# Moving 64 value matmuls of the cross attention from the last layer's network stage into the recurrence of the first layer

## The reference

```python
x = _layernorm(x + _L0_attn_ref(x, ...))        # selective state-space recurrence
x = _layernorm(x + _L0_xattn_ref(x, ctx, ctx))  # autocorrelation
x = _layernorm(x + _L0_ffn_ref(x, ...))         # quantized weights and LoRA
x = _layernorm(x + _L1_attn_ref(x, ...))        # 4-layer network with a scan
x = _layernorm(x + _L1_xattn_ref(x, ctx, ...))  # grouped-query cross attention
x = _layernorm(x + _L1_ffn_ref(x, ...))         # routed low-rank experts
```

```python
k_, v_ = jnp.split(kv @ Wkv + bkv, 2, axis=-1)   # kv = ctx; 8 heads of 128 each
```

## Time and profile before

| | us |
|---|---|
| time, median of 3 runs (1371.46 to 1374.9) | 1371.84 |
| span of the profiled execution | 1371.0 |
| PE busy | 1271.2 |
| DVE busy | 920.7 |
| ACT busy | 731.0 |
| POOL busy | 646.6 |
| recurrence: first scan starts, last scan ends | 136.7, 488.0 |
| network: first L801, last L835 starts | 673.0, 809.5 |
| first scores of the attention (L931) | 846.7 |

### The profile page before, as it was taken

One profiled execution on the slowest core, in us unless ns is written; L12 is line 12 of the kernel. 1 busy time (PEld: TensorE's weight loads), 2 busy tenths in 40 slices (PEclk: granted clock), 3 DMA queues, 4 the chain that ended last, 5 costly groups with the idle time before them and its releaser, 6 DMA issues.

```text
span 1371.0 us, 18309 instructions
## 1 busy us (share of the span) xinstructions
PE 1271.2 (93%) x6432; PEld 923.8 (67%) x6432; DVE 920.7 (67%) x1690; ACT 731.0 (53%) x1407; POOL 646.6 (47%) x471
## 2 busy tenths in 40 slices
PE   6996888888889989999999999999998999999996
PEld 5875766666677754444655556778787888888774
DVE  4774999999999877886644544544444464555566
ACT  5479999999998831112222234544444435444441
POOL 4128999999989702216511123533332543333221
PEclk9998899999999999999999999999999999999998
DMA  5002200040000060002110002212121222221110
GB/s 180 9 25 93 93 1 1 32 153 2 1 1 0 1 187 16 8 9 92 70 31 8 15 24 70 93 62 77 63 77 46 70 77 72 69 68 63 39 54 31
DMA packets 29641, 71.45 MB, mean 52 GB/s; under 512 B 3408, under 2 KB 3664, under 8 KB 27632
## 3 DMA queue, kind: packets, MB, share of 16 engines
q1 hardware_dynamic: 29552, 70.30, 15.6%
HBM read 68.12 MB, written 2.16 MB: 51 GB/s over the span
## 4 chain that ended last, share of the span: by engine, by line
PE 69%; DVE 10%; POOL 9%; issue 6%; ACT 4%; DMA 1%; DVEq 0%; SPq 0%; POOLq 0%; ACTq 0%
PE psum L502 10%; PE psum L504 9%; PE psum L503 9%; POOL arena L1420 8%; PE psum L931 4%; PE psum L791 4%; PE psum L958 4%; DVE arena L1696 4%; PE psum L785 3%; PE psum L602 3%; PE psum L577 3%; ACT arena L983 3%; PE psum L591 2%; PE psum L688 2%; PE psum L672 2%
## 5 line engine op out<-in xcount | busy, mean ns | idle before, releaser
L1356 POOL TENSOR_TENSOR w_split<-arena,w_split 128x512 fp32r<-128x512 f32 x128 | 168.0, 1331 | 315.1 <-ACT w_split L983 315.1
L1420 POOL TENSOR_TENSOR arena<-arena 128x1024 f32<-128x1024 f32 x128 | 300.4, 2373 | 28.3 <-DVE arena L1696 28.1
L1696 DVE TENSOR_TENSOR_SCAN arena<-psum,arena 128x512 f32<-128x512 f32 x256 | 290.6, 1200 | 15.7 <-ACT psum L983 15.5
L577 PE MATMUL psum<-prm,arena 128*128 128x128 f32 x1024 | 159.0, 284 | 59.1 <-DVE arena L1696 31.1
L577 PEld LDWEIGHTS psum<-prm,arena 128*128 128x128 f32 x1024 | 114.5, 143 | 121.1 <-issue 53.7
L983 ACT ACTIVATE arena<-psum,ssmC 128x256 f32<-128x256 f32 x448 | 179.9, 497 | 16.7 <-PE psum L577 16.6
L983 ACT ACTIVATE arena<-arena 128x512 f32<-128x512 f32 (+2 forms) x86 | 64.1, 749 | 224.9 <-DVE arena L1979 224.0
L983 ACT ACTIVATE psum<-arena,amat 128x508 f32<-128x508 f32 x256 | 172.3, 727 | 10.0 <-DVE arena L1696 10.0
L983 ACT ACTIVATE arena<-psum 128x512 f32<-128x512 f32 (+2 forms) x164 | 92.3, 575 | 154.7 <-PE psum L791 48.0
L983 ACT ACTIVATE arena<-psum,prm 128x512 f32<-128x512 f32 (+1 forms) x130 | 90.5, 708 | 133.4 <-PE psum L504 70.5
L591 PE MATMUL psum<-prm,arena 128*128 128x128 f32 x1024 | 135.0, 275 | 0.1
(11 more groups left out here) (225 smaller groups left out, 2353.3 us busy)
## 6 DMA issues: line engine op xcount, KB each, us to landing
arena<-wq SPq DMA_DIRECT2D x64, 256.0 KB, 2.5
arena<-wo SPq DMA_DIRECT2D x64, 256.0 KB, 2.9
arena<-bc_scratch SPq DMA_DIRECT2D x8, 1024.0 KB, 4.6
arena<-win SPq DMA_DIRECT2D x16, 256.0 KB, 4.2
arena<-xT SPq DMA_DIRECT2D x8, 256.0 KB, 7.1
x_tok<-xtok SPq DMA_DIRECT2D x1, 2048.0 KB, 10.2
arena<-wout SPq DMA_DIRECT2D x8, 256.0 KB, 5.8
arena<-ctxtok SPq DMA_DIRECT2D x1, 2048.0 KB, 7.9
```

The costliest lines, as they stand in the source:

```text
L577: last = nc.tensor.transpose(hT[:, c, b % 2, e, :], hst[:, (2 * k + e) % 4, b * L:(b + 1) * L], ident)
L1356: gp.tensor_tensor(out_, whole, hi.bitcast(F32), ALU.subtract).then_inc(done, 1)
L1420: gp.tensor_tensor(bu[:, i % 4, :, :], dtu[:, (2 * j + e) % 4, :].unsqueeze(1).to_broadcast([P, NG, HT]), Brep[:, q * NG:(q + 1) * NG, :], ...
L1696: v.tensor_tensor_scan(hst[:, i % 4, :], bank[decay_slot(i)][:, :], bu[:, (k // NG * 2 + e) % 4, k % NG, :], 0.0, ALU.mult, ALU.add).then_ ...
```

## The change

Five edits:
1. **Values in the recurrence.** The 64 value matmuls leave the network. In rounds 5 to 84 each group of five rounds makes one unit: a matmul into bank 5 in four rounds, after `sum_state`, and in the fifth a DVE copy of the bank to SBUF (`value_out`, ring of 3 in `row`), which SP stores to the device-memory tensor `v_keep`. The weights `wv` lie in `x_tok`, the context in a ring of two. `x_tok` is loaded after the last unit. `V` comes back from `v_keep` with one 4 MB load (fp32 128 x 8 x 1024) once the autocorrelation is done.
2. **The fourth decay buffer** is no PSUM bank any more (bank 5 is taken) but an SBUF tensor, `spare` (which later holds `dwout`); all 128 rounds have four buffers. So every scan with i % 4 == 3, 64 of 256, reads both its inputs from SBUF.
3. **Keys in smaller pieces**: `KV_PLAN` gives the matmuls by place: 12 a layer (4, 2, 4, 2), 4 ahead of layer 0, 12 in the tail, none between the queries.
4. `wk` comes after the feed-forward instead of after the autocorrelation's weights; the loads of `wo` no longer wait for the value units.
5. SP's queue in the recurrence is rearranged: replicas of B, context tokens, `wout` between the stores of the values.

```diff
@@ recurrence, SP
+            for q in range(4):
+                sp.wait_ge(S.dt_done, 4 * (q + 1))
+                replicas(0, q)
+                if q == 1:
+                    sp.wait_ge(S.inproj, len(UNITS))
+                    load(val_w, wv, S.val_in)
+                    value_tokens(0)
+                    value_tokens(1)
+            for n in range(2 * B):
+                if 9 <= n < 13:
+                    sp.wait_ge(S.bu_done, 2 * ((MP - 1) * GS + 2 * (n - 9) + 2))
+                    replicas(1, n - 9)
+                if n == 13:
+                    sp.wait_ge(S.skip_used, MD)
+                    sp.wait_ge(S.dtu_done, MD)
+                    for m in range(MD):
+                        load(wout_sb[:, m, :], wout[m], S.wout_in)
+                if n:
+                    sp.wait_ge(S.v_out, 16 * n)
+                sp.wait_ge(S.v_sb, n + 1)
+                sp.dma_start(v_keep[n // 2, :, n % 2 * 512:(n % 2 + 1) * 512],
+                             val_out[:, n % 3, :]).then_inc(S.v_out, 16)
+                if n % 2 and n // 2 + 2 < B:
+                    value_tokens(n // 2 + 2)
+            load(x_tok[:, :, :], xtok, S.xtok_in)
@@ network, SP
-            sp.wait_ge(S.wn_done, B)
+            sp.wait_ge(S.xat_done, B)
+            load(V, v_keep.rearrange("b p n -> p b n"), S.val_in)
+            sp.wait_ge(S.ffn_done, B)
             for i in range(NKV):
-                if i == 2:
-                    sp.wait_ge(S.h0_done, 2)
-                    load(wv_sb, wv, S.wv_in)
...
@@ PE
+            def value_piece(n, k):
+                if k == 0:
+                    if n == 0:
+                        pe.wait_ge(S.val_in, 16)
+                    else:
+                        pe.wait_ge(S.v_sb, n)
+                    pe.wait_ge((S.vx_in0, S.vx_in1)[n // 2 % 2], 16 * (n // 4 + 1))
+                last = mm(bank[5][:, :], val_x[:, n // 2 % 2, k, :], val_w[:, k, n % 2 * 512:(n % 2 + 1) * 512],
+                          start=(k == 0), stop=(k == KD - 1))
+                if k == KD - 1:
+                    last.then_inc(S.v_ps, 1)
@@ rounds, PE
                 if k:
                     sum_state(k - 1)
+                if val_step(k) and val_step(k)[1] < KD:
+                    value_piece(*val_step(k))
@@ ACT
-                if decay_free(i):
-                    act.wait_ge(S.scan_done, decay_free(i))
+                if i >= 4:
+                    act.wait_ge(S.scan_done, i - 3)
                 c = M % MD * NS + n
-                av(bank[decay_slot(i)][:, :].rearrange("p (b t) -> p b t", b=HB)[:, :, 1:],
+                av(decay_bank(i).rearrange("p (b t) -> p b t", b=HB)[:, :, 1:],
@@ DVE
+            def value_out(n):
+                dve.wait_ge(S.v_ps, n + 1)
+                if n >= 3:
+                    dve.wait_ge(S.v_out, 16 * (n - 2))
+                v.tensor_copy(val_out[:, n % 3, :], bank[5][:, :]).then_inc(S.v_sb, 1)
...
                 scan(2 * k + 1)
+                if val_step(k) and val_step(k)[1] == KD:
+                    value_out(val_step(k)[0])
@@ helpers
+        def decay_bank(i):
+            return spare[:, :] if i % 4 == 3 else bank[i % 4][:, :]
+        def val_step(k):
+            at = k - VAL_AT
+            return (at // VAL_STEP, at % VAL_STEP) if 0 <= at < 2 * B * VAL_STEP else None
+KV_PLAN = {0: 4, KV_LAST: 4, KV_LAST + 1: 4, KV_LAST + 2: 4}
+for _l in range(4):
+    KV_PLAN.update({1 + _l * KVL: 4, 1 + _l * KVL + 2: 2, 1 + _l * KVL + 3: 4, 1 + _l * KVL + 7: 2})
```

More of the change, by code:

```diff
@@ L214, in decoder_kernel @@
         zeros = sb("zeros", [P, 3 * HB])
+        spare = sb("spare", [P, HT])
+        val_w = x_tok[:, :, :].rearrange("p b d -> p (b d)").rearrange("p (k n) -> p k n", k=KD)
+        val_x = part(152, 2 * 512).rearrange("p (s k t) -> p s k t", s=2, k=KD)
+        val_out = row[:, 2 * P:2 * P + 3 * 512].rearrange("p (s n) -> p s n", s=3)
         bu = part(32, 4 * NG * HT).rearrange("p (s n t) -> p s n t", s=4, n=NG)
@@ L371, in emptied, with kv_pieces @@
             return S.in_evac, GATE_AT[i, h] + 1
[L373 to L379, removed]
+        def decay_bank(i):
[3 more added lines that the diff above has]
+            return (at // VAL_STEP, at % VAL_STEP) if 0 <= at < 2 * B * VAL_STEP else None
+        def kv_pieces(at):
+            before = sum(c for a, c in KV_PLAN.items() if a < at)
+            return range(before, before + KV_PLAN.get(at, 0))
         def by_dve(k, c):
@@ L437, in _, with replicas, value_tokens @@
[L437 to L440, removed]
+            def replicas(h, q):
+                load(Brep[:, q * 4:(q + 1) * 4, :].rearrange("p n t -> p (n t)"),
+                     scratch[h, q * 4:(q + 1) * 4, :].rearrange("n t -> (n t)").partition_broadcast(P),
+                     (S.b_in0, S.b_in1, S.b_in2, S.b_in3)[q])
+            def value_tokens(b):
+                load(val_x[:, b % 2, :, :], ctxT[:, b // HB, :, (b % HB) * L:(b % HB + 1) * L],
+                     (S.vx_in0, S.vx_in1)[b % 2])
@@ L802, in _ @@
                     last.then_inc(S.d_tr, 1)
-                    keys_values(1 + KVL * l + h)
+                    keys(1 + KVL * l + h)
                 for h in range(2):
@@ L848, in _ @@
             last_turn(0)
-            keys_values(KV_LAST, 0)
+            keys(KV_LAST)
             last_turn(1)
@@ L852, in _ @@
                 network_out(b)
-            keys_values(KV_LAST, 1)
-            keys_values(KV_LAST + 1)
+            keys(KV_LAST + 1)
             NU = 2 * NKV
@@ L868, in _ @@
             turn_half(0, 1, 1)
-            keys_values(KV_LAST + 2, 0)
+            keys(KV_LAST + 2)
             turn_half(0, 2, 0)
@@ L1105, in _ @@
             act.wait_ge(S.dt_base, 2 * MD)
-            av(bank[5][:, :].rearrange("p (s t) -> p s t", t=L)[:, :, 0:1], zeros[:, 0:HB].unsqueeze(2), ACT.Identity)
+            av(spare[:, :].rearrange("p (s t) -> p s t", t=L)[:, :, 0:1], zeros[:, 0:HB].unsqueeze(2), ACT.Identity)
             def decay(i):
```

128 lines of the change are left out of this document (48 added, 80 removed).

## The result

The changed kernel takes 1408.18 us (median of 4 runs, 1401.03 to 1412.37) against 1372.69 before: a ratio of 1.025 (95% interval 1.0231 to 1.027), slower. The profiled execution took 1407.51 with a span of 1405.7. The forecast was 1387 with a range of 1376 to 1405: the sign was right, and the loss of 35.5 us was more than twice the 15 us forecast.

A forecast was written before the change was run, and what follows sets the result against it. PE was taken to bound the network, four nearly full engines the recurrence, with POOL setting its pace after the change. 1371.8 - 34 (network) - 1 (tail) + 50 (recurrence) = 1386.8, forecast 1387 us, range 1376 to 1405.

The forecast's parts named there:

- The sign: Whole kernel: slower, 1387 us against 1371.8; slower was given a chance of 0.73.
- the decay in SBUF: Recurrence: 64 scans with both inputs in SBUF and POOL exclude each other; the deciding term, cost 50 us (42 to 68).
- Rival A: Recurrence: the two-SBUF-input scan doesn't take POOL's port; recurrence +12, time 1349 us, faster; chance 0.15.
- POOL sets the pace: Recurrence: POOL, held off 1.08 us per SBUF scan, makes rounds about 3.05 us; DVE's wait is hidden in waiting for bu.
- POOL no longer runs two groups ahead: End of recurrence: the last scans are through by 540.5 us, when the next stage can start at the earliest.
- a common 50: Recurrence: one cost of 50 us (42 to 68), the next stage starting at 540.5 instead of 490.62.
- rival C: Recurrence: DVE becomes the bound too, its SBUF-scan waits adding 25 to 40 us; also network clock falls; 1412 to 1427; chance 0.10.
- The values: Recurrence: value matmuls and copies by themselves cost 10.6 to some 25 us, of which copies on DVE 10.6.
- The fourth buffer: Recurrence, rounds 84 to 127: a fourth decay buffer there gives back up to 5 us.
- The wait for the tables: After the recurrence: tables load from POOL's last bu on, landing 9.4 us after issue; next stage starts at 540.5 at the earliest.
- Network: Four network layers: without value units, 25.0 us a layer, 134.3 down to 100; saves 34 us (bounds 28 and 55).
- The tail: After the last layer: three units stay, two now whole instead of halves; net -1 us (bounds -7 and +2).

The follow-up runs named there:

- no_copy: Changed kernel with three PSUM decay buffers, none in SBUF; value matmuls kept, their copies, stores and waits left out, V filled with context: 1348.65 us, ratio 0.9827.
- three_banks_only: Kernel before the change with three PSUM decay buffers in all rounds, value units still in the network: 1373.22 us, ratio 0.9993.
- act_copy: Changed kernel with three PSUM decay buffers, none in SBUF, and the value copies on ACT behind the round's weighing: 1351.98 us, ratio 0.9842.
- copy_by_turns: Changed kernel with three PSUM decay buffers, none in SBUF; even value copies on DVE one round later, odd ones on ACT: 1355.4 us, ratio 0.9859.

## Why the prediction was wrong in size

**Right.** The sign, and with it that the decay in SBUF is the term that decides: undoing it alone makes the changed kernel 49 us faster. DVE's scan of two SBUF inputs and POOL do exclude each other; the rule of the Trainium skill, "SBUF — State Buffer", section "Who interferes with whom", that the prediction names holds for this scan as for the two elementwise kinds of the earlier trace rows. The trace agrees: 1.86 to 2.03 on average against 1.20, and each scan that met POOL ended about 1.08 after it. Rival A falls.

**The step that failed** is "POOL sets the pace, and DVE's wait lies in time in which it would wait for bu anyway". The prediction put the exclusion down as 63 x 1.08 = 68 us by which POOL is held off, and DVE's own wait as hidden. Measured, it is the other way round. POOL was held off by 124 x 0.25 = 31 us in its bu and some 3 in L1402; DVE waited 41, on the path; and POOL's idle time, meant to fall to 12, rose to 57.9. There was nothing for DVE's wait to hide in: DVE never waits for a bu in this stage. Two things had been overlooked. The earlier trace rows already said who leads: POOL's 28.3 us of idle time are waits for scans, for the ring holds only two groups. And the earlier trace rows said it again: POOL's last bu ends at 478.9, 9.1 us before the last scan ends at 488.0, with 7 of the last 8 scans still to end; that is nearly the whole ring, full to the end. After the change it is 540.9 against 550.0, the same 9.1, where the prediction had "POOL no longer runs two groups ahead".

**The sum again, with what was measured.** Decay in SBUF 46, not part of a common 50; values 18; together 64 of stretch, and a start 2.3 earlier. That is rival C's mechanism, to which the prediction gave 0.10. Its mark, POOL idle for 20 or more, came true; its price was too high, since a scan waits 0.64 on average and not 1.2.

**The values.** By themselves they were put at 10.6 to 25, and 18.2 is inside that. But the prediction let them vanish behind POOL. And PE, put at nothing since a round would need 2.55 of 2.64 (only rival A has 6 for it), cost 7 to 8. That an engine which stays below the round's length still adds to it is what no_copy shows; by which waits was not traced.

**The fourth buffer** was to give back up to 5; three_banks_only gives 0.

**The wait for the tables** (about 2 of the 50) isn't there: the spectra start 2.6 behind the last scan after as before.

**Network.** 34 forecast, 29.2 measured. The chain gave 25.0 a layer, a layer at full clock takes 25.5, PE idle 3.3 of it (forecast 3.5): 2 us of the difference. The other 3 are the clock: in two of the layers it falls to the lower level, 1.2 GHz, for one stretch (act_copy's four layers, none with a fall, take 101.9). The prediction had this under rival C only. As other executions of this network had none to three such falls, two is the luck of this one. The tail gave -0.3 for -1.

**The clock in the recurrence** was no term of the prediction. It was at its lower level for 20.5 us more than before, by the estimate above up to some 10 of the 64.

Left open: how much of the stretch is the clock's, why copy_by_turns is no better, and by which waits the value matmuls cost their 7 to 8.

## What to carry to other kernels

When two engines exclude each other, find out first which of them the other already waits for: a full ring behind an engine (here 9.1 us of finished bu at the end) says that it isn't the one that sets the pace, however busy it is, and then the wait counts on the other. Price a buffer by taking it away before paying for its replacement: the fourth one was worth nothing, its move to SBUF cost 46 us, and without it the same change wins 15 us, 23 with the copy a round later. In a stage where the engines are busy for 84 to 96% of the time, moved work can cost on each engine that it touches. And look where a window cuts: an idle time "before" a group may belong to its first instruction alone.

## What the runs showed of the hardware

- A scan with two SBUF inputs that was issued at the same moment as a GpSimd instruction waited for all of it (3.43 for 1.22). The record shows the wait as busy time, so no view lists it as idle. Whenever more than 0.2 us of the GpSimd instruction were left, the scan ended 1.08 to 1.09 us after it (41 scans of the changed kernel). Scans with one input in PSUM stayed at 1.20 in every kernel.
- TensorE's granted clock falls in some layers of the network and not in others, at the same work. Three stretches of the changed kernel: ahead of a fall, in it, and at the end of an earlier layer, which had none:

```profile
785.40:788.80 3.40, 1.50 (x7) 0.87 (x7) 2.89 (x14) 1.10 (x2) 1.11 (x1) 1.00 0.00 0
```
```profile
788.80:792.20 3.40, 3.40 (x5) 1.36 (x5) 2.84 (x4) 0.37 (x1) 0.00 (x0) 0.51 0.00 0
```
```profile
759.00:762.20 3.20, 1.30 (x4) 0.23 (x3) 2.95 (x14) 0.69 (x1) 1.81 (x2) 1.00 0.16 56
```

  PE was busy for 1.50 of 3.40 us before it fell, and for 1.30 of 3.20 where it didn't; before the change the same place had 3.32 of 3.50 and no fall. The two layers with a fall took 1.7 and 1.5 us longer (the last one takes 25.4 in act_copy). What decides was not tried.
